# Last aggregation stage of a fused graph network: float32 records of 144 columns, or rounded and remainder parts of 288 in one float32r product

## The chip, the cores and the metric

The kernel runs on one core of one Trainium2 chip. The metric is the device time of one execution in microseconds; the median of three runs of the kernel before is 2964.3 us.

## The reference, cut to what matters

The whole kernel computes four graph layers on 3125 nodes (128 features) and 53125 edges. The change lies in the sums over edges that layers 3 and 4 share:

```python
# layer 3 (a GCN): sum over the edges of one sender block of rows
norm = deg_inv_sqrt[row] * deg_inv_sqrt[col]
agg = jax.ops.segment_sum(norm[:, None] * x[col], row, num_segments=n)
x = _layernorm(x + agg @ W.T + b)
# layer 4: mean of the 16 edge attributes over the edges of one sender
rec_attr = _scatter_mean(edge_attr, row, N)
h = concatenate([x, rec_attr, sent_attr], axis=1) @ W1 + b1
x = _layernorm(x + leaky(h) @ W2 + b2)
```

Both sums run over the same edges in the same order, so one matrix product with 128 + 16 = 144 columns makes both.

## The kernel before, in words

The order of every engine's work is written out by hand, engine by engine, with counted semaphores between them. The program is one long sequence of stages; the last stages are:

1. **Spreading the targets** (`spread_target`, L1245, on TensorE; `target_hot`, L2236, on VectorE; `keep_target`, L1516, on ScalarE): the target rows of layer 3 are spread over 149 windows and written to DRAM by indirect DMAs of GpSimd (L836). These 149 DMAs are the last work that GpSimd has.
2. **The sums**, which the change touches. 125 tiles (`NQ`), five to each of 25 sender blocks of 126 nodes. Tile `i` has 4 x 128 edges. SyncE loads it with two DMAs into one of six buffers `grec` (L720: 512 feature columns; L721: 64 attribute columns). VectorE builds four one-hot matrices of 128 x 126 (`slot_hots`, L2214, three tiles ahead). TensorE multiplies each one-hot matrix with the 144 columns of its slot (L1289) and adds all 20 products of a block up in one PSUM bank.
3. When a block is done, VectorE scales it out of PSUM (`keep_block`, L2221 for 128 columns, L2222 for 16), TensorE turns it around (`turn`, L1276 and L1278), and every four blocks VectorE adds the result to `acc` (`add_chunk`, L2227) and ScalarE keeps the attribute rows (L1534).
4. **The tail**: layer norm, the two dense products of layer 4, the last layer norm and the store.

The features of a record lie as (m, s, a): nine groups of 64 columns, each with four slots of 16, so that one slot's 144 columns are nine runs of 16 at a pitch of 64. VectorE's order in the stage is: four one-hots for each tile, `keep_block(b-1)` behind the second tile of block b, `add_chunk` behind the fifth tile of every fourth block.

Of the kernel before, what the change touches and what calls it, by code (L numbers as in the profile page):

```python
# [12 lines left out]

F32 = mybir.dt.float32
I32 = mybir.dt.int32
U8 = mybir.dt.uint8
ALU = mybir.AluOpType
# [13 lines left out]
CB = 4  # L31
# [41 lines left out]
YN = YW * WD  # L73
NYB = NU // YN
YU = -(-NYB // CB)
XO, GR, GH = RS, XS, 3
DST_AT, MEAN_AT = 86, 92
NORM_AT = {2: 6, 3: 22, 4: 38, 5: 54, 6: 70}
THOT_AHEAD = 3
# [71 lines left out]
def graph_kernel(nc, xT_d, dst_rows_d, dst_d, src_d, typ_d, mark_d, w_d, b_d, iota_d, out_d):  # L151
    with ExitStack() as ctx:
# [103 lines left out]
        with ExitStack() as slot_buffers:  # L256
# [22 lines left out]
            with ExitStack() as gcn_buffers:  # L279
                def three(name, shape, dt=F32):  # L280
                    return gcn_buffers.enter_context(nc.sbuf_tensor(name, shape, dt))

                yrows = three("yrows", [P, NYB, P])
                trow = three("trow", [P, NS, YW * SPAN], U8)
                thot = three("thot", [P, SS, SPAN])
                xo = three("xo", [P, XO, RECORD_COLS])
                grec = three("grec", [P, GR, 4 * (P + A)])
                ghot = three("ghot", [P, GH, 4, BS])
                gcn_lo = three("gcn_lo", [P, NTILE])
                sums = three("sums", [P, 2, P + A])  # L290

# [136 lines left out]
        def record_got(eng, i):  # L428

            s = i % GR  # L430
            eng.wait_ge(q(f"x1_stored_{s}"), 16 * (4 * len(range(s, NQ, XS)) + 2 * (i // GR + 1)))

        def record_put(eng, v):

# [121 lines left out]
        def _(eng):  # L556
# [159 lines left out]
            attrs_sent(eng, 4)  # L716
            for i in range(NQ):
                if i >= GR:
                    eng.wait_ge(q("gcn_sum"), i - GR + 1)
                eng.dma_start(grec[:, i % GR, 0:4 * P], x1_d[i * P:(i + 1) * P, 0:4 * P]).then_inc(q(f"x1_stored_{i % GR}"), 16)  # L720
                eng.dma_start(grec[:, i % GR, 4 * P:], attr_d[i * 4 * P:(i + 1) * 4 * P, :].rearrange("(p j) a -> p (j a)", j=4))\  # L721
                   .then_inc(q(f"x1_stored_{i % GR}"), 16)
# [10 lines left out]
        def _(eng):  # L733
# [100 lines left out]
            for v in range(NW):  # L834
                after(eng, "x1_evac", 5, v + 1)
                eng.indirect_dma_start(x1_d, bass.IndirectOffsetOnAxis(ap=put_idx[:, v:v + 1], axis=0), xo[:, v % XO, :], None)\  # L836
                   .then_inc(q(f"rec_got_{v % XO}"), 16)
            general(GCN)


        @block.tensor
        def _(eng):
# [438 lines left out]
            for i in range(NQ):  # L1281
# [1 line left out]
                if first_tile and b >= 2:  # L1283
                    eng.wait_ge(q("sums_kept"), b - 1)
                eng.wait_ge(q("ghot"), i + 1)
                record_got(eng, i)
                for j in range(4):
                    got = grec[:, i % GR, :].rearrange("p (m s a) -> p s m a", s=4, a=A)[:, j]
                    last = mm(ps[0:BS, 6 + b % 2, 0:P + A], ghot[:, i % GH, j, :], got, start=first_tile and j == 0,  # L1289
                              stop=last_tile and j == 3)  # L1290
                last.then_inc(q("gcn_sum"), 1)
                if i % QS == 2 and b >= 1:
                    turn(b - 1)
# [33 lines left out]
        def _(eng):  # L1327
# [193 lines left out]
            for kind, n in stage1_steps():  # L1521
# [7 lines left out]
                    ln_deviation(1, n)  # L1529
                elif kind == "unit":  # L1530
                    keep_target_rows(n)
            for c in range(NCH):
                eng.wait_ge(q("turn_mm"), min(c * CB + CB, TB))
                act(chunk(nodes, c)[SRC_ROWS], ps[SRC_ROWS, 3 + c % 2, 0:width(c)], ACT.Copy).then_inc(q("turn_used"), 1)  # L1534
            centered_square(2, 0)
            for c in range(3):
                centered_square(2, c + 1)
# [20 lines left out]
        def _(eng):  # L1558
# [658 lines left out]
            def keep_block(b):  # L2217
                eng.wait_ge(q("gcn_sum"), (b + 1) * QS)
                if b >= 2:
                    eng.wait_ge(q("turn_mm"), b - 1)  # L2220
                vec.tensor_scalar(sums[0:BS, b % 2, 0:P], ps[0:BS, 6 + b % 2, 0:P], dinv[0:BS, b:b + 1], None, ALU.mult)  # L2221
                vec.tensor_scalar(sums[0:BS, b % 2, P:], ps[0:BS, 6 + b % 2, P:P + A], deg[0:BS, 3, b:b + 1], None, ALU.mult)\  # L2222
                   .then_inc(q("sums_kept"), 1)

            def add_chunk(c):
# [144 lines left out]
```

## Time and profile before

| what | value |
|---|---|
| three runs | 2952.74, 2964.3, 2971.47 us |
| profiled execution, span from first to last instruction | 2969.2 us, mean TensorE clock 0.913 |
| the stage of the sums, first product to last | 2782.2 to 2921.5 us |
| busy over the whole span | TensorE 84%, VectorE 61%, ScalarE 29%, GpSimd 53% |
| DMA queues | 520 MB, 175 GB/s on average |

The span is what the profiler saw between the first and the last instruction of one execution. The time of that same execution outside the profiler isn't listed; its span lies 4.9 us above the median of the runs and inside their range. In the stage of the sums, unlike in the rest, GpSimd has no work and ScalarE has seven instructions.

### The profile page before, as it was taken

To read this page: it belongs to the slowest core of one execution; us is meant where nothing else is said; L and a number is where in the kernel's file an instruction comes from. 1 tells how busy PE (TensorE), PEld (TensorE's weight loads), DVE (VectorE), ACT (ScalarE), POOL (GpSimd) and SP (SyncE) were. 2 spreads that over 40 slices of the span, in tenths; PEclk is the share of its full clock that TensorE was granted. 3 is DMA by queue.
4 is the path that set the end of the run, shared out by engine and by line. 5 is a ranking of instruction groups with operands and counts; after the bars stand their busy time and mean duration, and the time that the engine had idled before them with its cause. 6 is when DMAs were issued, how large, how long until landed. Compare 5 with 4: busy or idle time off the path is not lost.

```text
span 2969.2 us, 45704 instructions
## 1 busy us (share of the span) xinstructions
PE 2492.2 (84%) x15625; PEld 2211.7 (74%) x15625; DVE 1808.3 (61%) x6126; ACT 868.5 (29%) x1546; POOL 1585.9 (53%) x1706
## 2 busy tenths in 40 slices
PE   7587878888687899746999998998989897878798
PEld 3366666666387889436999997888988886777797
DVE  4565656575576777423876655676865554433585
ACT  2355555554354111213222231111311110443102
POOL 0656666663577666542566626666456665565200
PEclk9789888888799999857999999999999999898899
DMA  7312112110398666106888887877788774565793
GB/s 273 111 50 53 51 51 53 51 52 25 103 281 260 166 173 170 38 27 210 274 272 270 269 266 231 240 228 211 238 273 251 226 234 134 174 213 198 232 267 105
DMA packets 271515, 520.11 MB, mean 175 GB/s; under 512 B 61999, under 2 KB 115554, under 8 KB 270501
## 3 DMA queue, kind: packets, MB, share of 16 engines
q1 hardware_dynamic: 185053, 289.49, 31.2%
q0 software_dynamic: 86224, 227.59, 26.6%
q8 instruction: 132, 2.16, 0.3%
q14 instruction: 106, 0.87, 0.1%
HBM read 323.93 MB, written 192.99 MB: 174 GB/s over the span
## 4 chain that ended last, share of the span: by engine, by line
PE 69%; issue 10%; DMA 7%; DVE 6%; another core or an unknown queue 4%; ACT 2%; POOL 2%; SPq 0%; DVEq 0%; POOLq 0%; ACTq 0%
PE ps L1058 21%; PE ps L1030 10%; PE ps L892 7%; PE ps L1043 6%; PE ps L1245 5%; PE ps L1289 4%; PE ps L886 4%; PE ps L878 4%; DMA chunks<-xs 2%; DMA rec<-chunks,idx 2%; DMA srow<-lanes_of_slots 1%; DVE shot L2033 1%; POOL attributes L744 1%; PE ps L1112 1%
## 5 line engine op out<-in xcount | busy, mean ns | idle before, releaser
L735 POOL DMA_INDIRECT rec<-chunks,idx x596 | 588.5, 987 | 500.5 <-PE ps L1058 184.9
L1058 PE MATMUL ps<-dhot,rec 128*128 128x168 f32 x4768 | 757.2, 312 | 70.4 <-issue 35.3
L1058 PEld LDWEIGHTS ps<-dhot,rec 128*128 128x128 f32 x4768 | 703.8, 194 | 99.6 <-issue 77.6
L2054 DVE TENSOR_SCALAR dhot<-iota,dcode 128x168 f32<-128x168 f32 x2384 | 584.6, 311 | 216.7 <-remote 102.4
L1030 PE MATMUL ps<-hrow,shot 126*128 126x128 f32 x4000 | 516.3, 284 | 63.8 <-issue 29.5
L735 POOL DMA_INDIRECT msg<-messages,idx_buf x416 | 398.2, 957 | 307.3 <-issue 189.7
L1030 PEld LDWEIGHTS ps<-hrow,shot 126*128 126x128 f32 x4000 | 493.7, 199 | 81.7 <-issue 65.9
L1386 ACT ACTIVATE xs<-ps 128x512 f32<-128x512 f32 x500 | 295.1, 597 | 763.5 <-PE ps L1030 393.8
L744 POOL DMA_INDIRECT attributes<-w,rank_to x352 | 353.2, 1004 | 213.1 <-issue 102.2
L2033 DVE TENSOR_SCALAR shot<-srow,lane_no 126x512 f32<-126x512 uint8 x500 | 230.2, 486 | 117.4 <-PE ps L1030 51.2
L892 PE MATMUL ps<-big,lane1h 128*128 128x300 f32 x832 | 231.6, 432 | 9.3 <-issue 8.0
L836 POOL DMA_INDIRECT chunks<-xo,put_idx x149 | 148.8, 999 | 119.7 <-ACT xo L1516 80.3
L892 PEld LDWEIGHTS ps<-big,lane1h 128*128 128x128 f32 x832 | 158.6, 196 | 69.6 <-issue 24.6
L1245 PE MATMUL ps<-yrows,thot 126*128 126x128 f32 (+1 forms) x1192 | 167.1, 302 | 41.9 <-ACT xo L1516 26.4
L878 PE MATMUL ps<-onehot,msg 128*128 128x128 f32 x832 | 129.9, 294 | 84.3 <-issue 83.6
L1364 ACT ACTIVATE tmp<-iota,slot_col 128x300 f32<-128x300 f32 x416 | 186.4, 530 | 33.3 <-DVE slot_col L1701 29.6
L1245 PEld LDWEIGHTS ps<-yrows,thot 126*128 126x128 f32 (+1 forms) x1192 | 158.3, 215 | 50.0 <-ACT xo L1516 29.9
L1043 PE MATMUL ps<-agg_rows,w 128*128 128x252 f32 (+1 forms) x832 | 185.5, 374 | 8.7 <-issue 8.2
L878 PEld LDWEIGHTS ps<-onehot,msg 128*128 128x128 f32 x832 | 117.1, 206 | 93.2 <-issue 93.0
L1043 PEld LDWEIGHTS ps<-agg_rows,w 128*128 128x128 f32 x832 | 153.1, 193 | 29.9 <-issue 13.7
L1676 DVE TENSOR_SCALAR onehot<-iota,dst_lo 128x128 f32<-128x128 f32 x416 | 88.4, 297 | 126.6 <-remote 124.7
L2099 DVE TENSOR_TENSOR agg_rows<-ps,tmp 128x504 f32<-128x504 f32 (+1 forms) x150 | 100.9, 673 | 99.5 <-PE ps L1058 51.3
(304 smaller groups left out, 2538.6 us busy)
## 6 DMA issues: line engine op xcount, KB each, us to landing
chunks<-xs SPq DMA_DIRECT2D x375, 256.0 KB
tmp<-inverse_counts SPq DMA_DIRECT2D x36, 1008.0 KB
chunks<-xs SPq DMA_DIRECT2D x125, 258.0 KB
srow<-lanes_of_slots SPq DMA_DIRECT2D x100, 320.0 KB
grec<-chunks SPq DMA_DIRECT2D x125, 256.0 KB
messages<-big SPq DMA_DIRECT2D x25, 504.0 KB
trow<-lanes_of_targets SPq DMA_DIRECT2D x30, 320.0 KB
rec<-chunks,idx POOLq DMA_INDIRECT x596
```

What stands on the lines that cost most here:

```text
L735: eng.indirect_dma_start(buf, None, table, bass.IndirectOffsetOnAxis(ap=index, axis=0)).then_inc(sem, 16)
L744: eng.indirect_dma_start(attr_d, bass.IndirectOffsetOnAxis(ap=rank_to[:, c:c + 1], axis=0), attr_rows(k, n // G)[:, n % G * TC + T:(n % G ...
L878: last = mm(ps[:, g % 2, 0:P], msg[:, g % SUB, t, :], onehot[:, g % 2, t, :], start=t == 0, stop=t == G - 1)
L892: last = mm(ps[:, 7, near_col(g):near_col(g) + NEAR], lane1h[:, g % 2, t, :], big[:, g % 2, t * NEAR:(t + 1) * NEAR], start=False, stop=Fa ...
L1030: last = mm(ps[:, STAGE1_BANKS[i % 3], j * P:(j + 1) * P], shot[0:BS, i % SS, j * P:(j + 1) * P], hrow[0:BS, sb_, :], start=True, stop=True)
L1043: last = mm(out, wt(REL[k], T)[:, t * P:(t + 1) * P], agg[gi % 2][:, t, 0:c1 - c0], start=t == 0, stop=k == 1 and t == T - 1)
L1058: last = mm(ps[:, 4 + i % 2, (v % 3) * WT:(v % 3 + 1) * WT], rec[:, v % RS, j * P:(j + 1) * P], dhot[:, v % DS, j * WT:(j + 1) * WT], star ...
L1245: last = mm(ps[:, STAGE1_BANKS[v % 3], j * P:(j + 1) * P], thot[0:nodes_of(c), v % SS, j * P:(j + 1) * P], yrows[0:nodes_of(c), c, :], sta ...
L1364: last = act(away[:, t * NEAR:(t + 1) * NEAR], iota[:, near_col(g):near_col(g) + NEAR], ACT.Abs, scale=-1.0, bias=slot_col[:, g % SUB, t:t ...
L1386: act(xs[:, i % XS, 0:4 * P], ps[:, STAGE1_BANKS[i % 3], :], ACT.Copy).then_inc(q("x1_evac"), 1)
L2033: vec.tensor_scalar(shot[0:BS, i % SS, :], srow[0:BS, s_ % NS, (n % QS) * SPAN:(n % QS + 1) * SPAN], lane_no1[0:BS], None, ALU.is_equal).t ...
L2054: last = vec.tensor_scalar(dhot[:, v % DS, j * WT:(j + 1) * WT], iota[:, 0:WT], dcode[:, v, j:j + 1], None, ALU.is_equal)
```

## The change: what it does

Every record is split into two halves before the product. ScalarE copies the 576 columns of a tile into `parts[..., 0, :]`, a float32r tile, in slot order; a float32r tile holds values that are rounded to fewer bits of mantissa. GpSimd subtracts that copy from the record and writes the remainder to `parts[..., 1, :]`, also float32r. The one-hot matrices become float32r too (ones and zeros lose nothing). TensorE then multiplies each one-hot matrix with 288 columns (rounded part and remainder side by side) in one float32r product, where before it had one float32 product of 144. `keep_block` first copies the remainder's sums out of PSUM, adds the rounded part's sums, and then scales; four VectorE instructions where two stood.

```diff
+F32R = mybir.dt.float32r
-XO, GR, GH = RS, XS, 3
+XO, GR, GH, GP = RS, XS, 3, 3
+GW_COLS = P + A
...
-                ghot = three("ghot", [P, GH, 4, BS])
+                ghot = three("ghot", [P, GH, 4, BS], F32R)
+                parts = three("parts", [P, GP, 4, 2, GW_COLS], F32R)
...
+        def record_by_slot(i):
+            return grec[:, i % GR, :].rearrange("p (m s a) -> p s m a", s=4, a=A)
+        def part_by_slot(i, half):
+            return parts[:, i % GP, :, half, :].rearrange("p s (m a) -> p s m a", a=A)
... SyncE
                 if i >= GR:
-                    eng.wait_ge(q("gcn_sum"), i - GR + 1)
+                    eng.wait_ge(q("part_low"), i - GR + 1)
... GpSimd
+            for i in range(NQ):
+                eng.wait_ge(q("part_high"), i + 1)
+                eng.tensor_tensor(part_by_slot(i, 1), record_by_slot(i), part_by_slot(i, 0).bitcast(F32), ALU.subtract)\
+                   .then_inc(q("part_low"), 1)
... TensorE
-                record_got(eng, i)
+                eng.wait_ge(q("part_low"), i + 1)
                 for j in range(4):
-                    last = mm(ps[0:BS, 6 + b % 2, 0:P + A], ghot[:, i % GH, j, :], got, start=first_tile and j == 0,
-                              stop=last_tile and j == 3)
+                    last = mm(ps[0:BS, 6 + b % 2, 0:2 * GW_COLS], ghot[:, i % GH, j, :],
+                              parts[:, i % GP, j, :, :].rearrange("p a b -> p (a b)"),
+                              start=first_tile and j == 0, stop=last_tile and j == 3)
... ScalarE
+            for i in range(NQ):
+                record_got(eng, i)
+                if i >= GP:
+                    eng.wait_ge(q("gcn_sum"), i - GP + 1)
+                act(part_by_slot(i, 0), record_by_slot(i), ACT.Copy).then_inc(q("part_high"), 1)
+                if i % QS == 4 and i // QS % CB == 0 and i // QS >= CB:
+                    keep_turned(i // QS // CB - 1)
... VectorE, keep_block
-                vec.tensor_scalar(sums[0:BS, b % 2, 0:P], ps[0:BS, 6 + b % 2, 0:P], dinv[0:BS, b:b + 1], None, ALU.mult)
-                vec.tensor_scalar(sums[0:BS, b % 2, P:], ps[0:BS, 6 + b % 2, P:P + A], deg[0:BS, 3, b:b + 1], None, ALU.mult)\
+                got = ps[0:BS, 6 + b % 2, :]
+                st.did(vec.tensor_copy(sums[0:BS, b % 2, :], got[:, GW_COLS:2 * GW_COLS]))
+                st.settle()
+                st.did(vec.tensor_tensor(sums[0:BS, b % 2, :], got[:, 0:GW_COLS], sums[0:BS, b % 2, :], ALU.add))
+                st.settle()
+                vec.tensor_scalar(sums[0:BS, b % 2, 0:P], sums[0:BS, b % 2, 0:P], dinv[0:BS, b:b + 1], None, ALU.mult)
+                vec.tensor_scalar(sums[0:BS, b % 2, P:], sums[0:BS, b % 2, P:], deg[0:BS, 3, b:b + 1], None, ALU.mult)\
```

What stands on VectorE in the stage before, from the first one-hots on (L2214 builds one-hots, L2221 and L2222 are `keep_block`):

```order
L2214 TENSOR_SCALAR ghot<-iota,gcn_lo 128x126 x28
L2221 TENSOR_SCALAR sums<-ps,dinv 126x128
L2222 TENSOR_SCALAR sums<-ps,deg 126x16
L2214 TENSOR_SCALAR ghot<-iota,gcn_lo 128x126 x20
L2221 TENSOR_SCALAR sums<-ps,dinv 126x128
```

And the same place in the changed kernel (its L2239 are the one-hots, L2247 to L2252 `keep_block`):

```order
L2239 TENSOR_SCALAR ghot<-iota,gcn_lo 128x126 x28
L2247 COPY sums<-ps 126x144
L2249 TENSOR_TENSOR sums<-ps,sums 126x144
L2251 TENSOR_SCALAR sums<-sums,dinv 126x128
L2252 TENSOR_SCALAR sums<-sums,deg 126x16
L2239 TENSOR_SCALAR ghot<-iota,gcn_lo 128x126 x20
```

The number and the order of the one-hots stay; two instructions are added to each of 25 blocks.

What stands on ScalarE between the last kept target (L1516) and the tail before:

```order
L1516 ACTIVATE xo<-ps 128x4x8x16 x70
L1534 ACTIVATE nodes<-ps 16x504 x6
L1534 ACTIVATE nodes<-ps 16x126
L1450 ACTIVATE h<-acc 128x504 x2
L1454 ACTIVATE stat<-ps,bias 126x4
```

And in the changed kernel (its L1531 are the kept targets, L1555 the rounded copies, L1549 the attribute rows):

```order
L1531 ACTIVATE xo<-ps 128x4x8x16 x70
L1555 ACTIVATE parts<-grec 128x4x144 x25
L1549 ACTIVATE nodes<-ps 16x504
L1555 ACTIVATE parts<-grec 128x4x144 x20
L1549 ACTIVATE nodes<-ps 16x504
```

ScalarE now has one copy for each of the 125 tiles. GpSimd, which had nothing behind its last indirect DMA (the changed kernel's L847), gets one subtraction for each tile (L851):

```order
L847 DMA chunks<-xo,put_idx 16768x516 x149
L851 ISA
L851 TENSOR_TENSOR parts<-grec,parts 128x4x144 x125
L561 TENSOR_LOAD bad_flag
L561 ISA x2
```

TensorE keeps 20 products in each block and the two turns behind them; they read 288 columns instead of 144.

## Rows read from the trace of the kernel before

**Rows 1.** Windows of the stage: engines' busy time and count, granted clock, DMA share, GB/s.

```profile
core 0: us, PE busy (x) PEld busy (x) DVE busy (x) ACT busy (x) POOL busy (x), PEclk, DMA share, GB/s
2792.15:2921.50 129.35, 129.35 (x1006) 120.17 (x1005) 108.22 (x511) 3.49 (x6) 0.00 (x0) 1.00 0.90 260
```

**Rows 2.** Timeline of TensorE's products, two blocks: start, length, merged instructions.

```profile
2792.15 5.17 PE L1289 MATMUL ps<-grec,ghot 128*126 128x144 f32 x40
2797.68 5.17 PE L1289 MATMUL ps<-grec,ghot 128*126 128x144 f32 x40
2803.20 1.00 PE L1289 MATMUL ps<-grec,ghot 128*126 128x144 f32 x6
```

**Rows 3.** Timeline of VectorE in one block of the stage.

```profile
2793.44 0.87 DVE L2214 TENSOR_SCALAR ghot<-iota,gcn_lo 128x126 f32<-128x126 f32 x4 [0.73 <-PE ps L1289]
2794.42 0.35 DVE L2221 TENSOR_SCALAR sums<-ps,dinv 126x128 f32<-126x128 f32 x1
2794.68 0.23 DVE L2222 TENSOR_SCALAR sums<-ps,deg 126x16 f32<-126x16 f32 x1
2794.83 3.40 DVE L2214 TENSOR_SCALAR ghot<-iota,gcn_lo 128x126 f32<-128x126 f32 x16
```

**Rows 4.** Groups of VectorE by line and shape, whole span: busy us, mean ns.

```profile
L2214 DVE TENSOR_SCALAR ghot<-iota,gcn_lo 128x126 f32<-128x126 f32 x500 | 103.9, 280 | 28.9 <-PE ps L1289 27.1
L2130 DVE TENSOR_TENSOR tmp<-h,tmp 128x504 f32<-128x504 f32 x12 | 8.2, 683 | 9.4 <-ACT tmp L1466 7.0 <-issue 2.3
L2130 DVE TENSOR_TENSOR tmp<-h,tmp 128x126 f32<-128x126 f32 x2 | 0.6, 292 | 0.9 <-ACT tmp L1466 0.9
L2137 DVE COPY acc<-ps 128x126 f32<-128x126 f32 x2 | 0.6, 290 | 4.7 <-issue 4.7
L2145 DVE TENSOR_TENSOR x<-acc,ps 128x126 f32<-128x126 f32 x4 | 1.1, 277 | 1.0 <-issue 1.0
L2227 DVE SCALAR_TENSOR_TENSOR acc<-ps,bias,x 128x504 f32<-128x504 f32 x6 | 4.5, 742 | 3.2 <-PE ps L1278 3.2
```

**Rows 5.** ScalarE copies out of SBUF, groups by shape.

```profile
L1450 ACT ACTIVATE h<-acc 128x504 f32<-128x504 f32 x12 | 7.3, 618 | 9.3 <-DVE acc L2294 8.0 <-DVEq L2275 1.3
L1450 ACT ACTIVATE h<-acc 128x126 f32<-128x126 f32 x2 | 0.6, 303 | 2.5 <-DVE acc L2294 2.5
```

**Rows 6.** GpSimd's copies, one line: duration ns min/median/max.

```profile
L796 POOL COPY xs<-code x125: 176/194/758, 798.5 to 962.3; 128x4 f32<-128x4 f32 x125
```

**Rows 7.** Timeline, GpSimd and VectorE around 896 us.

```profile
895.64 0.54 POOL L796 COPY xs<-code 128x4 f32<-128x4 f32 x1 [1.74 <-DMA chunks<-xs]
896.33 1.51 POOL L744 DMA_INDIRECT attributes<-rec,rank_to  x1 [0.15 <-issue]
897.84 0.20 POOL L796 COPY xs<-code 128x4 f32<-128x4 f32 x1
...
895.58 0.55 DVE L1958 TENSOR_SCALAR dhot<-agg_rows,lane_no 128x650 f32<-128x650 f32 x1
896.17 0.81 DVE L1959 TENSOR_TENSOR agg_rows<-dhot 128x625 f32<-128x625 f32 x1
897.01 0.81 DVE L1960 TENSOR_TENSOR tmp<-tmp,agg_rows 128x625 f32<-128x625 f32 x1
897.86 1.49 DVE L1961 TENSOR_REDUCE dhot<-tmp 128x25 f32<-128x625 f32 x1
```

**Rows 8.** Timeline, GpSimd and VectorE around 818 us.

```profile
817.92 1.17 POOL L744 DMA_INDIRECT attributes<-w,rank_to  x1
818.65 0.67 DVE L2033 TENSOR_SCALAR shot<-srow,lane_no 126x512 f32<-126x512 uint8 x1 [0.41 <-PE ps L1030]
819.54 0.48 DVE L2033 TENSOR_SCALAR shot<-srow,lane_no 126x512 f32<-126x512 uint8 x1 [0.22 <-PE ps L1030]
```

**Rows 9.** Timeline of SyncE's queue at the stage's start: the first loads.

```profile
2779.23 0.32 SPq L720 DMA_DIRECT2D grec<-chunks  x1
2779.60 0.43 SPq L721 DMA_DIRECT2D grec<-attributes  x1
2780.08 0.42 SPq L720 DMA_DIRECT2D grec<-chunks  x1
2780.55 0.43 SPq L721 DMA_DIRECT2D grec<-attributes  x1
```

More of the change, by code:

```diff
@@ L1285, in _ @@
                 eng.wait_ge(q("ghot"), i + 1)
-                record_got(eng, i)
+                eng.wait_ge(q("part_low"), i + 1)
                 for j in range(4):
-                    got = grec[:, i % GR, :].rearrange("p (m s a) -> p s m a", s=4, a=A)[:, j]
-                    last = mm(ps[0:BS, 6 + b % 2, 0:P + A], ghot[:, i % GH, j, :], got, start=first_tile and j == 0,
-                              stop=last_tile and j == 3)
+                    last = mm(ps[0:BS, 6 + b % 2, 0:2 * GW_COLS], ghot[:, i % GH, j, :],
+                              parts[:, i % GP, j, :, :].rearrange("p a b -> p (a b)"),
+                              start=first_tile and j == 0, stop=last_tile and j == 3)
                 last.then_inc(q("gcn_sum"), 1)
@@ L1531, in _, with keep_turned @@
                     keep_target_rows(n)
-            for c in range(NCH):
+            def keep_turned(c):
                 eng.wait_ge(q("turn_mm"), min(c * CB + CB, TB))
                 act(chunk(nodes, c)[SRC_ROWS], ps[SRC_ROWS, 3 + c % 2, 0:width(c)], ACT.Copy).then_inc(q("turn_used"), 1)
+            for i in range(NQ):
[5 more added lines that the diff above has]
+                    keep_turned(i // QS // CB - 1)
+            for c in range((TB - 1) // CB, NCH):
+                keep_turned(c)
             centered_square(2, 0)
```

## The prediction

> **What bounds the kernel now.** I read the windows of the stage of the sums first, since only this stage changes. From 2792.15 to 2921.50 us TensorE is busy 129.35 of 129.35 us at the full granted clock, VectorE 108.22, ScalarE 3.49, GpSimd nothing; the DMA share is 0.90 [rows 1]. So TensorE sets the pace. The timeline then gives the pace: a block of five tiles starts every 5.53 us (2792.15, 2797.68, 2803.20), of which 5.17 are 40 product instructions, two to a product [rows 2]. That is 5.17 / 20 = 0.26 us a product, 0.07 us a tile for the turns, **1.105 us a tile**, 125 tiles. The engines beside it have little room. VectorE's one-hots go at 3.40 / 16 = 0.212 us each [rows 3], 0.85 a tile. The loads share 0.90 at 1.105 us, so they would be full at about 1.105 x 0.90 = 0.99 us a tile; SyncE issues one load in 0.475 us (2779.60 to 2780.08 to 2780.55, [rows 9]), two to a tile, 0.95 us. Even a free product could take no more than some 0.11 to 0.15 us off a tile, 14 to 19 us of the whole.
>
> **The change part by part.**
>
> *TensorE.* A product has 288 columns instead of 144 in another type. No row has a float32r product. If a column costs what it costs now, it takes twice as long, 0.52 us. The other end comes from the same row: one of the two instructions takes 5.17 / 40 = 0.129 us for 144 columns, and at the granted 2.4 GHz that is 310 cycles, two to a column and a little over; a single instruction with one cycle to a column would be through with 288 columns in 0.12 to 0.13 us. A tile takes 4 x 0.13 + 0.07 = 0.59 us at one end and 4 x 0.52 + 0.07 = 2.14 us at the other. I take the lower end, since a type that holds less is what the two halves are cut for; at half the clock it is 1.11 us, still no more than now.
>
> *ScalarE.* One copy of 576 columns a tile: 618 ns for 504 columns and 303 for 126 [rows 5] make 0.83 ns a column, so 0.68 us. It runs three tiles ahead and is hidden below any pace over 0.75 us. Behind its wait for `gcn_sum` stand its own next copy and, every 20 tiles, the attribute rows; nobody else.
>
> *VectorE.* A block had 0.35 + 0.23 us of `keep_block`, on the timeline 0.4 beyond the one-hots [rows 3]. Now: a copy of 144 columns out of PSUM, 290 ns for 126 plus 18 more, 0.31; the addition, 277 ns plus 18 more columns, 0.30; the two scalings, now out of SBUF, 0.28 (the 126 column one-hot) and about 0.20 [rows 3, 4]. That is 1.09 us a block. With 20 x 0.212 = 4.25 and a quarter of `add_chunk`'s 0.742 [rows 4] VectorE has 5.52 us a block, **1.105 us a tile**: by itself as slow as TensorE is now. So whatever TensorE saves, the stage doesn't get faster; I exclude a gain beyond what the estimate of these four instructions may be off, 0.05 us a tile or 6 us.
>
> *GpSimd.* One subtraction of 576 columns with two SBUF inputs a tile. The trace has no GpSimd arithmetic, only copies of 4 columns, 194 ns in the median [rows 6]. The nearest row by operation is VectorE's subtraction of two SBUF tiles, 683 ns for 504 columns and 292 for 126, or 1.037 ns a column [rows 4]. Lower bound: GpSimd is as fast as that, 0.76 us. Upper bound: it moves its three streams one behind the other at that rate, 3 x 576 x 1.037 = 1.79 us, plus the 0.19 of an almost empty instruction, 1.98 us. I take two streams (it fetches one input, then the other, and writes beside that): 1.195 + 0.19 = **1.39 us**, in the middle between the ends. That alone is more than 1.105.
>
> The Trainium skill ("GPSIMD Engine Reference", section 3.1) gives 4497 ns for a GpSimd addition of two float32 tiles with 2048 columns; scaled to 576 that is an estimate of 1.27 us, and the sum below would be some 15 us lower. No row here shows it.
>
> *GpSimd and VectorE together.* The trace shows that they exclude each other in some instructions. A 4 column copy on GpSimd that usually takes 0.19 us took 0.54 when it began at 895.64 beside a VectorE TENSOR_SCALAR of 650 columns that ended at 896.13; it ended at 896.18. An indirect DMA of GpSimd took 1.51 us beside two TENSOR_TENSORs and ended at 897.84, 20 ns behind the second. The next copy, beside a TENSOR_REDUCE, took 0.20 [rows 7]. So an instruction of GpSimd stands still until a VectorE instruction of the first two kinds is through, and VectorE instructions of the third kind don't matter. The one-hots are of the first kind: TENSOR_SCALAR, SBUF to SBUF. The other direction shows only faintly: a one-hot of 0.48 us took 0.67 beside an indirect DMA [rows 8]. If a long GpSimd instruction holds VectorE off in the same way, their times add up. Per tile: four one-hots, 0.85; the two scalings out of SBUF, (0.28 + 0.20) / 5 = 0.10; GpSimd's streams, 1.195, with its 0.19 of start beside VectorE's work: **2.145 us a tile**. With GpSimd's bounds that is 0.76 + 0.95 = 1.71 and 1.98 + 0.95 = 2.93.
>
> The Trainium skill ("SBUF — State Buffer", section "SBUF: two separate sides") has VectorE and GpSimd share one pair of ports as an exclusive lock for the whole instruction, in both directions, and counts VectorE instructions in a two-port mode or with two SBUF inputs among them. The trace agrees for GpSimd's side, with the 0.54 us above; for VectorE's side no row here decides it.
>
> *Ends.* At the start a record now passes ScalarE and GpSimd before the first product: 0.68 + 1.39 = 2.1 us. At the end the last tile's products come behind GpSimd (up to 1.0 us) and the last `keep_block` is 0.55 us longer. Together 3.7 us. The waits of SyncE now hang on `part_low` rather than `gcn_sum`; six tiles of buffer cover them at any pace above 0.99 us.
>
> **Sum.** 125 x (2.145 - 1.105) = 130.0, plus 3.7, is 133.7 us on the profiled span of 2969.2 us. That span lies 4.9 us over the median of the runs, so I put the difference on the median: 2964.3 + 133.7 = **3098 us**.
>
> **The rivals.**
>
> *A. VectorE isn't held off.* GpSimd waits for the rest of a one-hot (half of 0.28 us on average), but VectorE passes. For it: rows 8 show only 0.19 us lost on VectorE's side. Against it: an exclusion that works one way only would be odd. The pace is GpSimd's, 1.39 + 0.14 = 1.53 us: 125 x 0.425 + 3.7 = 57, **3021 us**. With GpSimd at 1.2 to 1.7 us in all it is 2980 to 3042.
>
> *B. Not slower: GpSimd is quick.* At VectorE's rate and without exclusion (0.76 us) VectorE itself is the bound at 1.105 us, and only the ends remain: **2968 us**. It decides below 1.1 us per subtraction, waiting included. For it speaks only that no row shows GpSimd slow; against it that the subtraction reads two inputs beside a VectorE that is busy 0.84 of the time [rows 1]. A gain over 1% would need 0.84 us a tile, under SyncE's and VectorE's own floor.
>
> *C. The product is no cheaper per column.* At 2.14 us a tile TensorE is the bound, whatever GpSimd does: 125 x 1.035 + 3.7 = 133, **3097 us**, the forecast's time by another road; then TensorE's busy time stays at 100% of the stage.
>
> *D. Both exclusion and GpSimd's upper bound.* 2.93 us a tile: 125 x 1.825 + 3.7 = 232, **3196 us**.
>
> **How the numbers follow.** Forecast 0.50, A 0.27, B 0.11, C 0.05, D 0.07. The range leaves out B and D (0.18) and a little of A's low end: 2985 to 3160 us, the upper end being 2.64 us a tile. One per cent, 30 us, is about what a measurement of this kernel can tell from no change. Slower by over 1% (above 2994): all but B and the low end of A, 0.83. Within 1%: 0.16. Faster by over 1%: 0.01. The likeliest case's own range is 3043 (1.71 us a tile) to 3160.
>
> **What would show it.** In the changed kernel's stage: a block of five tiles every 10.7 us; GpSimd's subtraction near 1.4 us when alone, its count 125; one-hots whose mean rises well above 280 ns or stand idle for the same time, in step with GpSimd; TensorE busy under half of the stage, released by GpSimd's `parts`; the DMA share near 0.5. A is right if the one-hots still take 0.28 us and GpSimd is busy without a gap at 7 to 8 us a block. B is right if a block takes 5.5 us and VectorE is full. C is right if TensorE is full. The prediction fails if GpSimd's subtraction is much off 1.4 us or its instructions and VectorE's overlap freely.

## The result, and the profile after

| | before | after |
|---|---|---|
| median of four runs | 2959.5 us (2952.7 to 2971.5) | 3090.0 us (3082.4 to 3095.8) |
| stage of the sums, start of first product to start of last | 2782.2 to 2921.2: 139.1 us | 2765.2 to 3029.4: 264.2 us |
| the same, per tile (125) | 1.11 us | 2.11 us |

After divided by before is 1.0427, with an interval of 1.0384 to 1.047: **130.5 us more**. The prediction said 133.7 more, 3098 us in all, in a range of 2985 to 3160. The execution of after that was profiled took 3082.4 us, and its span is 3080.5, 111.3 longer than the span of before. The stage makes +125.1 of that and the tail behind it +3.1 (51.1 us from the last product to the end, 48.0 before). The work ahead of the stage, which the change doesn't touch, was 17 us shorter in this one execution; such differences come from run to run.

The windows of the changed kernel first. The columns are those of [rows 1]: busy time and count of each engine, granted clock, DMA share, GB/s.

```profile
2800.00:2850.00 50.00, 30.11 (x115) 22.84 (x115) 45.72 (x120) 16.73 (x25) 31.66 (x23) 0.66 0.52 136
2850.00:2900.00 50.00, 29.70 (x105) 22.40 (x105) 46.28 (x114) 16.09 (x24) 31.18 (x23) 0.58 0.56 142
2900.00:2950.00 50.00, 28.01 (x105) 21.02 (x103) 46.93 (x109) 16.22 (x25) 33.46 (x24) 0.60 0.52 135
```

TensorE was busy without a gap; now it is busy 28 to 30 of 50 us, and the loads fell from 0.90 to 0.52. The fullest engine is VectorE, at 46 of 50 us, yet in these 50 us it does fewer instructions than before did (511 in 129 us [rows 1] are 198 in 50; here they are 109 to 120). So its instructions have become longer. GpSimd is busy 31 to 33 of 50.

The groups show which. The columns are line, engine, operation, operands, shapes, count, busy time, mean ns of one, and the engine's idle time before them with what ended it. From 2770 to 3045 us, nearly the stage:

```profile
L2239 DVE TENSOR_SCALAR ghot<-iota,gcn_lo 128x126 fp32r<-128x126 f32 x486 | 187.4, 460 | 13.8 <-PE ps L1303 13.8
L851 POOL TENSOR_TENSOR parts<-grec,parts 128x576 fp32r<-128x576 f32 x121 | 168.7, 1416 | 87.4 <-ACT parts L1555 87.4
L1303 PE MATMUL ps<-parts,ghot 128*126 128x288 f32 x488 | 138.1, 444 | 106.2 <-DVE ghot L2239 88.6 <-POOL parts L851 14.0 <-issue 3.6
L1555 ACT ACTIVATE parts<-grec 128x576 fp32r<-128x576 f32 x120 | 81.4, 684 | 145.3 <-PE ps L1303 144.9
L2252 DVE TENSOR_SCALAR sums<-sums,deg 126x16 f32<-126x16 f32 x25 | 21.9, 877 | 0.0
L2251 DVE TENSOR_SCALAR sums<-sums,dinv 126x128 f32<-126x128 f32 x25 | 17.2, 688 | 0.9
L2249 DVE TENSOR_TENSOR sums<-ps,sums 126x144 f32<-126x144 f32 x25 | 7.7, 307 | 0.9
L2247 DVE COPY sums<-ps 126x144 f32<-126x144 f32 x25 | 7.5, 301 | 1.7 <-PE ps L1303 1.1
```

The one-hot of 126 columns had a mean of 280 ns [rows 4] and now has 460. The two scalings out of SBUF take 688 and 877 ns; the copy and the addition beside them, which read PSUM, take what they should, 301 and 307. Single durations (shortest, median, longest) say how:

```profile
L2239 DVE TENSOR_SCALAR ghot<-iota,gcn_lo x500: 271/279/1504, 2749.4 to 3027.0; 128x126 fp32r<-128x126 f32 x167
L2252 DVE TENSOR_SCALAR sums<-sums,deg x25: 222/1386/1399, 2775.6 to 3030.6; 126x16 f32<-126x16 f32 x25
L851 POOL TENSOR_TENSOR parts<-grec,parts x125: 1383/1402/1485, 2763.7 to 3023.8; 128x576 fp32r<-128x576 f32 x125
```

Most one-hots still take 0.28 us. Some take up to 1.50, longer by 1.22 us, most of a subtraction's 1.40. The scaling of 16 columns takes 1.39 us in the median, for work of 0.22, so it waits 1.17. That is one engine standing still for the other, not both being somewhat slower. Here it is in one block, on the timeline (start, length, merged instructions, in brackets the idle time before and what ended it):

```profile
2835.36 3.01 PE L1303 MATMUL ps<-parts,ghot 128*126 128x288 f32 x12
...
2837.54 5.47 POOL L851 TENSOR_TENSOR parts<-grec,parts 128x576 fp32r<-128x576 f32 x4 [0.60 <-ACT parts L1555]
...
2838.37 0.67 DVE L2251 TENSOR_SCALAR sums<-sums,dinv 126x128 f32<-126x128 f32 x1
2838.95 1.39 DVE L2252 TENSOR_SCALAR sums<-sums,deg 126x16 f32<-126x16 f32 x1
...
2839.10 0.77 PE L1303 MATMUL ps<-parts,ghot 128*126 128x288 f32 x4 [0.73 <-POOL parts L851]
...
2840.26 5.57 DVE L2239 TENSOR_SCALAR ghot<-iota,gcn_lo 128x126 fp32r<-128x126 f32 x16
...
2843.54 1.33 PE L1303 MATMUL ps<-parts,ghot 128*126 128x288 f32 x4 [3.67 <-DVE ghot L2239]
...
2845.53 3.03 PE L1303 MATMUL ps<-parts,ghot 128*126 128x288 f32 x12
```

A block lasts 10.17 us here, from 2835.36 to 2845.53. Beside the same 16 one-hots that took 3.40 us before [rows 3] stand GpSimd's subtractions, up to 2843.01, and the 16 take 5.57 us: 2.17 more, while two subtractions fall into them. TensorE then waits 3.67 us for one-hots. The table of waits from 2790 to 3030 us (us in total, times, longest) names the same engine:

```profile
PE ps L1303 <- DVE ghot L2239: 82.5, 38, 3.7
PE ps L1303 <- POOL parts L851: 13.0, 17, 1.2
POOL parts L851 <- ACT parts L1555: 81.8, 59, 4.0
ACT parts L1555 <- PE ps L1303: 132.6, 91, 4.3
```

GpSimd waits too, for ScalarE's copies, and these wait for the buffers that TensorE frees. So no engine is busy without a gap in this stage: VectorE and GpSimd take turns, with a circle of waits around them.

### The profile page after: what moved, and what is told of

Same layout as the page of the kernel before. It is cut to its first block, busy times and chain, and to the rows that moved or that the text cites. A ratio compares the mean times of both kernels' runs of the same rounds, so it can differ in the third digit from the quotient of the medians.

```text
span 3080.5 us, 45128 instructions
## 1 busy us (share of the span) xinstructions
PE 2502.7 (81%) x15125; PEld 2192.4 (71%) x15125; DVE 1934.4 (63%) x6176; ACT 953.3 (31%) x1671; POOL 1769.5 (57%) x1831
## 4 chain that ended last, share of the span: by engine, by line
PE 58%; DVE 18%; issue 9%; another core or an unknown queue 6%; DMA 5%; ACT 2%; POOL 1%; DVEq 0%; SPq 0%; ACTq 0%; POOLq 0%
PE ps L1073 21%; PE ps L1045 10%; PE ps L1058 6%; PE ps L1260 5%; DVE ghot L2239 4%; PE ps L907 3%; DVE lane1h L1733 2%; PE ps L901 2%; PE ps L1303 2%; DMA chunks<-xs 2%; PE ps L893 2%; DMA rec<-chunks,idx 2%; DVE onehot L1701 1%; DVE shot L2058 1%
## 5 line engine op out<-in xcount | busy, mean ns | idle before, releaser
L1045 PE MATMUL ps<-hrow,shot 126*128 126x128 f32 x4000 | 509.5, 281 | 57.8 <-issue 29.4
L1045 PEld LDWEIGHTS ps<-hrow,shot 126*128 126x128 f32 x4000 | 486.9, 196 | 75.6 <-issue 56.8
L1303 PE MATMUL ps<-parts,ghot 128*126 128x288 f32 x500 | 142.0, 444 | 117.2 <-DVE ghot L2239 88.6
L851 POOL TENSOR_TENSOR parts<-grec,parts 128x576 fp32r<-128x576 f32 x125 | 174.1, 1415 | 93.1 <-ACT parts L1555 93.1
L1303 PEld LDWEIGHTS ps<-parts,ghot 128*126 128x126 f32 x500 | 113.7, 303 | 146.8 <-DVE ghot L2239 102.8
L847 POOL DMA_INDIRECT chunks<-xo,put_idx x149 | 149.0, 1000 | 118.1 <-ACT xo L1531 79.3
L2239 DVE TENSOR_SCALAR ghot<-iota,gcn_lo 128x126 fp32r<-128x126 f32 x500 | 192.5, 460 | 28.6 <-PE ps L1303 28.6
## 6 DMA issues: line engine op xcount, KB each, us to landing
chunks<-xs SPq DMA_DIRECT2D x125, 258.0 KB
```

The costliest lines, as they stand in the source:

```text
L1045: last = mm(ps[:, STAGE1_BANKS[i % 3], j * P:(j + 1) * P], shot[0:BS, i % SS, j * P:(j + 1) * P], hrow[0:BS, sb_, :], start=True, stop=True)
L1303: last = mm(ps[0:BS, 6 + b % 2, 0:2 * GW_COLS], ghot[:, i % GH, j, :], parts[:, i % GP, j, :, :].rearrange("p a b -> p (a b)"), start=firs ...
L2239: last = vec.tensor_scalar(ghot[:, i % GH, j, :], iota[:, 0:BS], gcn_lo[:, at:at + 1], None, ALU.is_equal)
```

## The experiments

The kernels ran in three sets, each on one chip with runs of the kernel before beside it. Chips differ: the kernel before had medians of 2996.7 us (the first four experiments), 2999.5 (the next four) and 2646.7 (the last three), against 2959.5 in the runs of the result. Every ratio is to the runs beside it. "Stage" is from the start of the first product to the start of the last, in the one execution that was profiled. The changed kernel's 264.2 us and the 139.1 of before come from the runs of the result, and the stages of all three sets are held against them. This can be checked: what stage and tail together are longer or shorter than in the kernel before agrees with the difference of the medians on the same chip within 10 us for every experiment, and within 2 us for the last three.

| run | median us | ratio (95%) | stage us |
|---|---|---|---|
| the change (first result) | 3090.0 | 1.0427 (1.0384 to 1.047) | 264.2 |
| one-hots read PSUM | 3067.2 | 1.0220 (1.0172 to 1.0268) | 201.6 |
| no subtraction | 2986.4 | 0.9962 (0.9926 to 0.9999) | 127.3 |
| half a subtraction | 3053.9 | 1.0196 (1.0153 to 1.0239) | 192.1 |
| before, subtraction beside it | 3120.4 | 1.0412 (1.0365 to 1.0459) | 267.2 |
| six buffers | 3114.6 | 1.0374 (1.0334 to 1.0414) | 253.0 |
| `keep_block` out of PSUM | 3122.6 | 1.0406 (1.0359 to 1.0454) | 258.0 |
| both out of PSUM | 3031.5 | 1.0120 (1.0081 to 1.0158) | 171.5 |
| before, PSUM one-hots, subtraction beside it | 3001.2 | 1.0000 (0.9968 to 1.0032) | 143.6 |
| before, four small pieces beside it | 2717.5 | 1.0273 (1.0241 to 1.0305) | 207.6 |
| the change, subtraction on VectorE | 2719.0 | 1.0271 (1.0244 to 1.0299) | 208.7 |
| before, a copy beside it | 2669.7 | 1.0092 (1.0059 to 1.0126) | 163.0 |

**One-hots read PSUM.** Only the place of VectorE's input changes.

```diff
+            st.do(vec.tensor_copy(ps[:, 5, 0:BS], iota[:, 0:BS]))
-  ... ghot[:, i % GH, j, :], iota[:, 0:BS], gcn_lo ...
+  ... ghot[:, i % GH, j, :], ps[:, 5, 0:BS], gcn_lo ...
```

> The changed kernel, but the one-hots read their row of numbers from PSUM instead of SBUF; nothing else differs. Theory X (GpSimd's subtraction and VectorE's SBUF-to-SBUF instructions exclude each other, so their times add up; the changed kernel has 2.11 us a tile): one-hots no longer stand still, the pace falls to 1.45 to 1.65 us a tile, the stage from 264 us to 181 to 206, the time to 3007 to 3032 us. Theory L (the round trip of three buffers through TensorE, ScalarE and GpSimd sets the pace): no change or a little slower, 3090 us. Theory V (VectorE's two added instructions a block set it): slower, since each one-hot out of PSUM takes longer.

Measured: 201.6 us, 62.6 less, although a one-hot by itself became longer. No one-hot waits any more (328, 334 and 352 ns for the shortest, the median and the longest). The exclusion is left where SBUF is still read, and there it grew:

```profile
L2239 DVE TENSOR_SCALAR ghot<-ps,gcn_lo 128x126 fp32r<-128x126 f32 x500 | 131.9, 335 | 18.3 <-PE ps L1303 18.2
L2252 DVE TENSOR_SCALAR sums<-sums,deg 126x16 f32<-126x16 f32 x25 | 33.5, 1339 | 0.0
L2251 DVE TENSOR_SCALAR sums<-sums,dinv 126x128 f32<-126x128 f32 x25 | 18.8, 751 | 0.9
```

**No subtraction.** From the fourth tile on GpSimd does nothing; TensorE and SyncE wait for ScalarE's copy instead. The remainders of later tiles are left out of the sums.

```diff
-            for i in range(NQ):
-                eng.wait_ge(q("part_high"), i + 1)
+            for s in range(GP):
+                eng.wait_ge(q("part_high"), s + 1)
... TensorE, SyncE
-                    eng.wait_ge(q("part_low"), ...)
+                    eng.wait_ge(q("part_high"), ...)
```

> The changed kernel without the subtraction from the fourth tile on: the remainder half of the product then holds the remainders of the first three tiles, so the sums lack their own remainders; the products keep 288 columns, ScalarE's copies and VectorE's four instructions a block stay. X: VectorE alone bounds the stage at 1.11 us a tile, 139 us, so the time is that of the kernel before within 8 us (2955 to 2970). V: the stage stays well above 1.3 us a tile (over 2985 us). If the float32r product were as dear per column as the float32 one: 2.1 us a tile, 3090 us.

Measured: 127.3 us, 1.02 us a tile, with 288 columns in every product and all of VectorE's additions, 12 us under the 139 that theory X expected. Its window:

```profile
2830.00:2880.00 50.00, 39.81 (x226) 29.29 (x226) 49.30 (x240) 35.71 (x55) 0.00 (x0) 1.00 0.98 295
```

TensorE is busy 0.80 of the time at the full clock, so the product is cheap. VectorE is busy 49.3 of 50 us and the DMA share is 0.98: the next two bounds stand here side by side. This is what the change would have brought with a remainder that costs nothing: 0.4% of the kernel (0.01 to 0.74% by the interval). Three rows from the stage, for the account below:

```profile
2851.38 1.34 PE L1306 MATMUL ps<-parts,ghot 128*126 128x288 f32 x8 [0.55 <-ACT parts L1558]
...
2862.63 4.00 DVE L2242 TENSOR_SCALAR ghot<-iota,gcn_lo 128x126 fp32r<-128x126 f32 x20
2866.55 0.30 DVE L2250 COPY sums<-ps 126x144 f32<-126x144 f32 x1
```

**Half a subtraction.** Two of the four slots, 288 of 576 columns, from the fourth tile on; the other remainders are left out.

```diff
-  eng.tensor_tensor(part_by_slot(i, 1), record_by_slot(i), ...
+  eng.tensor_tensor(part_by_slot(i, 1)[:, 0:2], record_by_slot(i)[:, 0:2], ...
```

> The changed kernel, but from the fourth tile on GpSimd subtracts two of the four slots (288 of 576 columns; the other two keep old remainders). GpSimd's instruction should take 0.19 + 1.2 / 2 = 0.8 us. X: 0.95 of VectorE plus 0.6 is 1.55 to 1.65 us a tile, the stage 194 to 206 us, 3020 to 3035 us. Rival P (the pace is GpSimd's alone or that of its chain, nothing adds up): 0.8 us is below the others' 1.11, so 2960 to 2970 us.

Measured: 192.1 us, just under what the theory had given it, and the one-hots' mean is 381 ns. The group of GpSimd gives the price by size:

```profile
L852 POOL TENSOR_TENSOR parts<-grec,parts 128x288 fp32r<-128x288 f32 x122 | 99.4, 822 | 86.3 <-ACT parts L1557 85.1
```

0.82 us for 288 columns and 1.40 for 576: 2.0 ns a column and 0.24 us fixed. The stage is 72.1 us shorter for 0.58 us less in each of 122 tiles, 70.8 us: it follows GpSimd's length one to one, though GpSimd stands idle for 86.3 us of it. That is what times that add up look like. A ring of waits that stands in no other engine's way could give the same slope; the next two experiments tell the two apart. Against the run without subtraction, the half one costs 64.8 us, 0.53 in each of the 122 tiles, and the whole one 136.9 us, 1.12.

**Before, subtraction beside it.** The kernel before, float32 products and all, plus one subtraction of 576 float32 columns a tile on tiles of its own. Nobody waits for it; only it waits, for `gcn_sum` and for its own last subtraction.

```diff
+                eng.wait_ge(q("gcn_sum"), i - 2)
+                eng.wait_ge(q("side"), i + 1)
+                eng.tensor_tensor(side[:, 2, 0:576], side[:, 0, 0:576], side[:, 1, 0:576], ALU.subtract).then_inc(q("side"), 1)
```

> The kernel before, with one float32 subtraction of 576 columns on GpSimd for each tile beside it, on tiles of its own in SBUF; it is let go by TensorE's count of finished tiles and nobody waits for it. X: VectorE's one-hots stand still for it, the stage grows from 139 us to 1.9 to 2.15 us a tile (238 to 269 us), the time to 3060 to 3090 us. L, V and P: nobody waits for GpSimd, so nothing changes: 2960 us.

Measured: 267.2 us. An instruction that nobody waits for, on an engine that was idle, nearly doubles the stage, as much as the whole change did (ratios 1.0412 and 1.0427). Its timeline:

```profile
2849.98 10.06 DVE L2222 TENSOR_SCALAR ghot<-iota,gcn_lo 128x126 f32<-128x126 f32 x20
...
2851.00 1.41 POOL L845 TENSOR_TENSOR side<-side 128x576 f32<-128x576 f32 x1 [2.21 <-PE ps L1297]
...
2852.92 6.05 POOL L845 TENSOR_TENSOR side<-side 128x576 f32<-128x576 f32 x4 [0.52 <-PE ps L1297]
```

Twenty one-hots need 20 x 0.212 = 4.25 us alone [rows 3]; beside five subtractions they take 10.06. So a subtraction takes 5.81 / 5 = 1.16 us away from VectorE, of its 1.41: about a quarter of a microsecond of it lies beside VectorE's work, as much as the fixed part above. (With 4.00 us for twenty one-hots, as in the run without subtraction, it is 1.21.) The single durations of the changed kernel say the same: a VectorE instruction waits 1.17 us (1.39 less 0.22) or at most 1.22 (1.50 less 0.28).

**Six buffers.** `parts` and the one-hots get six buffers instead of three, in space that earlier stages are done with.

```diff
-XO, GR, GH, GP = RS, XS, 3, 3
+XO, GR, GH, GP = RS, XS, 6, 6
```

> The changed kernel with six buffers instead of three for the parts and for the one-hots (they lie where the target rows lay, so the first one-hots start some 2 us later). X: the work that excludes each other adds up whatever the buffers: 2.0 to 2.15 us a tile, stage 250 to 269 us, 1.038 to 1.045 of the kernel before. L (round trip through three buffers): the pace falls towards GpSimd's 1.42 us, stage 178 to 200 us, 1.013 to 1.022.

Measured: 253.0 us, 11 less than the change. The circle of waits costs about that much; the other 114 us over the stage of before are not the buffers'. VectorE, busy 46 of 50 us in the changed kernel, now has hardly a gap:

```profile
2900.00:2950.00 50.00, 29.71 (x123) 24.09 (x124) 49.59 (x132) 15.06 (x24) 30.79 (x23) 0.66 0.54 142
```

**`keep_block` out of PSUM.** Two scalings straight out of PSUM, then two multiply-adds of PSUM and SBUF.

```diff
-  copy, addition, two scalings of sums
+  st.did(vec.tensor_scalar(sums[...0:P], got[:, two:two + P], dinv...))
+  st.did(vec.tensor_scalar(sums[...P:], got[:, two + P:2 * two], deg...))
+  vec.scalar_tensor_tensor(out=sums[...0:P], in0=got[:, 0:P], scalar=dinv..., in1=sums[...0:P], mult, add)
+  vec.scalar_tensor_tensor(out=sums[...P:], in0=got[:, P:two], scalar=deg..., in1=sums[...P:], mult, add)
```

> The changed kernel with keep_block written so that none of its four instructions goes from SBUF to SBUF with one input: two scalings out of PSUM, then two multiply-adds with one input in PSUM and one in SBUF. X: 0.48 us a block of shared time go, 0.10 us a tile, stage 248 to 254 us, total 10 to 15 us below the changed kernel. Rival W (while GpSimd has work queued, every such VectorE instruction waits out a whole subtraction, so the count of instructions decides, not their length): two of 22 waits a block go, 1.0 us a block, stage about 239 us, 25 us less.

Measured: 258.0 us, 6 less, a miss for both expectations; in the whole time the two kernels can't be told apart (1.0406 and 1.0427, intervals that overlap). The four instructions do what was meant (342, 220, 351 and 225 ns, none held up), but the one-hots' mean rose from 460 to 528 ns: what no longer waited in `keep_block` waited there.

```profile
L2239 DVE TENSOR_SCALAR ghot<-iota,gcn_lo 128x126 fp32r<-128x126 f32 x500 | 227.2, 528 | 20.6 <-PE ps L1303 20.6
L2253 DVE SCALAR_TENSOR_TENSOR sums<-ps,deg,sums 126x16 f32<-126x16 f32 x25 | 5.6, 225 | 0.0
```

**Both out of PSUM.** The first and the sixth edit together.

> Both: one-hots out of PSUM and keep_block out of PSUM. X: nothing of VectorE excludes GpSimd any more; the pace is GpSimd's own, 1.42 to 1.47 us a tile, stage 178 to 184 us (e1_iota_psum had 202), 1.012 to 1.017 of the kernel before; ScalarE's, VectorE's and GpSimd's instructions have their lone durations. If the 0.2 us a tile that e1_iota_psum had above GpSimd's pace come from the round trip: stage stays at 200 us.

Measured: 171.5 us, 30 less than with PSUM one-hots alone. It is a little less than expected. Now GpSimd runs almost without a gap, and a tile takes 1.37 us, as long as one of its subtractions:

```profile
2897.66 9.61 POOL L851 TENSOR_TENSOR parts<-grec,parts 128x576 fp32r<-128x576 f32 x7 [0.20 <-ACT parts L1555]
...
2898.80 5.21 DVE L2239 TENSOR_SCALAR ghot<-ps,gcn_lo 128x126 fp32r<-128x126 f32 x20
```

9.61 / 7 = 1.37 us each, beside 20 one-hots that run on at 5.21 / 20 = 0.26 us. This is the best version of the change that was found, and it is still 1.2% slower than the kernel before.

**Before, PSUM one-hots, subtraction beside it.** The fourth kernel with the first edit.

> The kernel before with the lone subtractions on GpSimd that nobody waits for (as e4_before_beside), and one-hots out of PSUM. X: VectorE is no longer held off; it needs 4 x 0.265 + 0.15 = 1.2 us a tile, stage 145 to 155 us, 1.002 to 1.006 of the kernel before. If GpSimd's reading slowed the stage by something else than VectorE's port (SBUF traffic of the loads or of TensorE): it stays above 1.6 us a tile, over 1.02.

Measured: 143.6 us, just below what was expected, against 267.2 with one-hots out of SBUF; ratio 1.0000. GpSimd still does its 125 subtractions, at 1417 ns, but at this pace it falls behind. 92 of them fall in the stage and some 32 beside the tail (time and count of these subtractions, clock, DMA share, GB/s):

```profile
2822.10:2965.70 143.60, 127.63 (x92) 0.98 0.87 255
2965.70:3020.00 54.30, 45.85 (x32) 0.80 0.08 30
```

At 1.16 us each the 92 would have cost VectorE some 107 us; the stage is 4.5 us longer than before's. So in the stage their price is gone with nothing changed but where VectorE reads 126 numbers. In the tail a part of it is left: VectorE's `tmp<-tmp` instructions there (L2298), with two SBUF inputs, take 1.19 us in the median and up to 1.54, instead of 0.68, and the tail takes 54.4 us instead of 48.0.

**Before, four small pieces beside it.** The fourth kernel, its subtraction cut into four of 144 columns.

```diff
+                for j in range(4):
+                    eng.tensor_tensor(side[:, 2, j * 144:(j + 1) * 144], side[:, 0, j * 144:(j + 1) * 144],
+                                      side[:, 1, j * 144:(j + 1) * 144], ALU.subtract).then_inc(q("side"), 1)
```

> The kernel before with the lone work of e4_before_beside cut in four: four subtractions of 144 columns for each tile instead of one of 576. From e3_half_sub (0.82 us for 288 columns) and the full one (1.41 for 576) a piece should take 0.53 us. X (held for the whole instruction, whichever engine starts first): the sum stays, 0.85 + 4 x (0.53 - 0.2) to 4 x 0.53, 2.15 to 2.95 us a tile, stage 265 to 370 us: no better than the 267 us of the uncut one. Rival (only long instructions hurt, VectorE slips in between short ones): stage under 220 us.

Measured: 207.6 us, 60 less than in one piece. The expectation that four starts would cost more than one failed.

```profile
2479.49 4.02 DVE L2224 TENSOR_SCALAR ghot<-iota,gcn_lo 128x126 f32<-128x126 f32 x10
2479.76 0.29 PE L1299 MATMUL ps<-grec,ghot 128*126 128x144 f32 x1
2480.07 3.80 POOL L846 TENSOR_TENSOR side<-side 128x144 f32<-128x144 f32 x8
```

Ten one-hots take 4.02 us here and eight pieces 3.80: the engines go almost in turn. A one-hot comes every 0.40 us, 0.19 later than alone, so a piece costs 10 x 0.19 / 8 = 0.24 us. The whole stage says nearly the same, but here too GpSimd falls behind VectorE; of the 500 pieces some 421 run in the stage, 3.4 a tile, and 71 behind it:

```profile
2457.90:2665.50 207.60, 164.90 (x1072) 135.61 (x1072) 204.65 (x542) 3.49 (x6) 192.17 (x421) 0.99 0.69 176
```

VectorE had 0.16 x 1.105 = 0.18 us a tile to spare [rows 1] and has none now (50.0 of 50 us from 2500 to 2650). The stage is 68.5 us longer than before's, 0.55 a tile, so 3.4 pieces take 0.73 us, 0.22 each, of their 0.49. By the same count the single subtraction takes at most 128.1 / 125 + 0.18 = 1.20 us of its 1.41 (VectorE still has gaps there, 45 to 46 of 50 us busy), near the 1.16 from the timeline. So about a quarter of a microsecond of every piece lies beside VectorE's work, and it isn't lost but hidden four times. Of the 60 us between the two stages a part is only work put off: with these 71 in it, at 0.22 us, the stage would take an estimated 223 us, still 44 less than 267.2.

**The change, subtraction on VectorE.** Behind each tile's four one-hots; GpSimd idle.

```diff
+                slot_hots(i)
+                eng.wait_ge(q("part_high"), i + 1)
+                vec.tensor_tensor(part_by_slot(i, 1), record_by_slot(i), part_by_slot(i, 0).bitcast(F32), ALU.subtract)
```

> The changed kernel with the subtraction on VectorE, behind each tile's one-hots, and GpSimd idle. X: nothing to exclude; VectorE has 0.85 + 0.76 + 0.22 + 0.04 = 1.87 us a tile, stage 232 to 238 us, 1.030 to 1.035 of the kernel before: 0.2 us a tile less than with the help of GpSimd. If GpSimd were any help, this kernel would be slower than the changed one (over 264 us).

Measured: 208.7 us; both ways of counting had said more.

```profile
2481.64 0.87 DVE L2235 TENSOR_SCALAR ghot<-iota,gcn_lo 128x126 fp32r<-128x126 f32 x4
2482.42 0.75 DVE L2291 TENSOR_TENSOR parts<-grec,parts 128x576 fp32r<-128x576 f32 x1
2483.09 0.87 DVE L2235 TENSOR_SCALAR ghot<-iota,gcn_lo 128x126 fp32r<-128x126 f32 x4
2483.87 0.75 DVE L2291 TENSOR_TENSOR parts<-grec,parts 128x576 fp32r<-128x576 f32 x1
```

Four one-hots and a subtraction repeat after 1.45 us, so the subtraction takes 1.45 - 0.78 = 0.67 of VectorE's time though its row says 0.75. One engine alone does the work of both in 209 us; the two together, getting in each other's way, need 264. (The two were timed on different chips, each against its own runs of before: 1.0271 and 1.0427.)

**Before, a copy beside it.** The fourth kernel with a copy of 576 columns, one SBUF input, in place of the subtraction.

> The kernel before with a GpSimd copy of 576 columns (one input) for each tile beside it, nobody waits for it. A copy should take about half of the subtraction, 0.2 + 0.6 = 0.8 us. X: it excludes the one-hots as well: 0.85 + 0.65 to 0.85 + 0.8, plus 0.1, 1.6 to 1.75 us a tile, stage 200 to 219 us. Rival (only two-input instructions of GpSimd need the shared way): stage 139 us as in the kernel before.

Measured: 163.0 us, between the 200 or more that the first theory expected and the 139 of the rival. The one-hots' mean is 375 ns and GpSimd's copy takes 719 ns: a GpSimd instruction with one input holds VectorE off as well. The stage is 23.9 us longer, 0.19 a tile; with the 0.18 to spare the copy takes 0.37 us of VectorE's time. The expectation had counted its whole length and nothing to spare.

## Why the prediction was right

**The mechanism** was that GpSimd's subtraction and VectorE's one-hots exclude each other in both directions, so that their times add up. It is shown: a subtraction that nobody waits for nearly doubles the stage (267.2 us), it stops doing so when the one-hots read PSUM (143.6, with 92 subtractions in it), and half the subtraction gives back half of its time (192.1). What stands still in these runs is VectorE. The other direction hardly shows in them: beside one-hots out of SBUF a subtraction takes 1.39 to 1.52 us ("before, subtraction beside it"), beside one-hots out of PSUM 1.40 to 1.41, so a one-hot costs GpSimd 0.11 us at most. That GpSimd waits out a VectorE instruction rests on [rows 7]. Against the product or VectorE's additions as the cause stands the run without subtraction (127.3), against missing buffers the run with six (253.0).

The Trainium skill ("SBUF — State Buffer", section "SBUF: two separate sides") has the two engines share a pair of ports as an exclusive lock in both directions, held for the whole instruction. The trace agrees for VectorE's side, which the rows of before had left open: its instruction of 16 columns took 1.39 us beside a subtraction, 0.22 without. On the whole length it does not quite agree: VectorE waits 1.17 to 1.22 us of a subtraction that the trace has at 1.40. The copy with one input, in the last run, excludes as well.

**Term by term.**

- *The tile.* 2.145 us predicted, 2.11 measured. That they come within 0.03 us is in part luck. The prediction had no term for the circle of waits, which is 11 us or 0.09 a tile; without it (six buffers) a tile takes 2.02 us, 0.12 less than the predicted sum. Every part of that sum was a little high. The one-hots, taken as 0.85, are 0.78 where nothing holds them up (3.92 us for 20, in the run without subtraction); the two scalings, taken as 0.10, are 0.07 (2852.42 to 2852.76 there); GpSimd's excluding part, taken as 1.195 of 1.39 us, measured 1.16 to 1.21 of 1.41. By these rows the sum is an estimated 2.01 to 2.06.
- *GpSimd's length.* 1.39 us predicted, 1.41 measured. The two streams were a choice in the middle of 0.76 to 1.98, from VectorE's rate; the measured 2.0 ns a column are twice VectorE's 1.03, so the choice fits, but nothing in the rows could have told it. The prediction's other estimate, 1.27 us, was 10% low. (The slope of [rows 4] is 1.034 ns, not 1.037, which changes the sum by 0.4 us; and the upper bound of 2.93 us counts GpSimd's 0.19 of start as excluding, where the middle case doesn't: 2.74 would be consistent.)
- *ScalarE.* 0.68 us predicted, 0.684 measured, hidden.
- *The product.* The lower end was nearly right: at the full clock four in a row take 0.77 us and eight 1.34, so 0.14 each beyond the run-out, against 0.12 to 0.13, and the kernel without subtraction ran 1.02 us a tile. Rival C, on TensorE at 2.14 us a tile, would have kept it full; it was busy 0.56 to 0.60 of the windows above. The prediction had a price for half the clock, 1.11 us a tile, but not that it would come. The clock is 1.00 in the stage of before and without the subtraction (TensorE busy 39.8 of 50 us), and 0.58 to 0.66, so most of the time at the 1.2 GHz level, in the changed stage, where TensorE waits up to 3.7 us at a time. At a granted clock of 0.50 (2782.2 to 2785.4 us) 12 products take 3.25 us and four 1.33, 0.24 each beyond the run-out. So "busy under half of the stage" came out wrong. What the slower products cost the stage was not measured by itself; the circle of waits that they stand in is worth 11 us.
- *VectorE by itself.* 1.105 us a tile predicted, and 1.02 measured at 49.3 of 50 us busy. Of the 0.42 us a block that were counted too much, 0.33 lie in the one-hots: 20 of them take 3.92 us up to the next instruction (2862.63 to 2866.55 above), where 20 x 0.212 = 4.25 had been counted from a row that ends with the last one's run-out. The four instructions of `keep_block` were counted by their rows' durations, 1.09 us, and take 1.02, since each starts before the one ahead has ended. So the gain that the prediction excluded beyond 6 us was there, 12 us of stage (139.1 to 127.3), and rival B's 2968 us should have been some 12 us lower.
- *`keep_block`'s two scalings out of SBUF.* 0.10 us a tile predicted, 12 us in all. Taking them away gave 6 us beside one-hots out of SBUF and 30 beside one-hots out of PSUM. As I read it, they have no price of their own, and an instruction that waits at the port costs what the others leave it; no run tests that reading.
- *Who is named.* I expected TensorE's idle time to be ended by `parts`; it was ended by `ghot`, 82.5 to 13.0 us. Both engines hold each other up here, so which of them is named last did not tell the cause.
- *The ends.* 3.7 us predicted. From the issue of the first load to the first product it takes 5.1 us (2760.1 to 2765.2) instead of 3.0 (2779.2 to 2782.2), 2.1 more, as predicted. The tail took 3.1 more, but hardly for the reason given, a longer last `keep_block`: with the same `keep_block`, in the kernel without subtraction, it takes 48.4 us, 0.4 more than before, while the kernel before with a subtraction beside it, whose `keep_block` is the old one, has 51.0. What goes with the long tails is TensorE's granted clock, 0.80 against 0.86. The windows of the tails, of the kernel before and of the kernel before with a subtraction beside it:

```profile
2921.20:2969.20 48.00, 40.58 (x198) 29.23 (x196) 19.41 (x45) 14.93 (x36) 0.00 (x0) 0.86 0.09 34
3064.60:3115.60 51.00, 43.55 (x198) 31.10 (x196) 19.50 (x45) 14.95 (x36) 0.00 (x0) 0.80 0.09 32
```

- *The others.* A block 10.57 us on average (10.7 predicted), a DMA share of 0.52 to 0.56 (0.5), 125 subtractions of 1.40 us (1.4).

Rival A, GpSimd waiting and VectorE not, falls with the one-hots of 1.5 us. D falls with GpSimd's 1.40.

**Still open.** Why the scalings gave 6 us in one setting and 30 in the other was read from where the waits went, not tested further. How the fixed part of a GpSimd instruction lies in time, ahead of its hold on the port or behind it, wasn't tried; nor were pieces inside the change itself. No run looks at how a float32r tile rounds, on which the split into two parts rests.

## What to carry to other kernels

Before an idle GpSimd is given elementwise work, count what VectorE does in the same stretch out of SBUF: their times add up, and the engine that looked free costs most of its length (1.16 of 1.41 us for a subtraction, 0.37 of 0.72 for a copy). If the work must go there, let VectorE's instructions read PSUM (0.26 us a one-hot instead of 0.21, and 62.6 us less of stage), or do it on VectorE itself (208.7 us instead of 264.2); here both were still slower than no change. And before the fullest engine is relieved, read what stands right behind it: here VectorE, the loads and their issue stood within 0.18 us of the 1.105 of a tile, so that even a remainder for nothing would have brought 0.4%.

## What the runs showed of the hardware that was not expected

- A float32r product of 288 columns takes 0.24 us at the lower clock level (3.25 us for 12, 1.33 for four, at a granted clock of 0.50) and 0.14 at the full one (1.34 us for eight, 0.77 for four). A float32 one of 144 is two instructions of 0.129 us each at the full level [rows 2].
- GpSimd's subtraction with two SBUF inputs: 0.49, 0.82 and 1.41 us for 144, 288 and 576 columns, the same for float32r and float32 results, for runs of 16 columns and for contiguous ones.
- A VectorE instruction of 16 columns out of SBUF can take 1.39 us when GpSimd holds the port. Several short instructions of GpSimd cost VectorE less than one long one of the same columns: 0.22 to 0.24 us for each 144, against 1.16 for 576.
